# Denominators from the exponentials' accumulator, projections in pairs, and rows normalised ahead, in a two-layer decoder kernel

## The reference, cut to what matters

```python
# routed feed-forward: 64 experts, 3 per row, 128 rows each
logits = xf @ gate_w + gate_b
top_l, top_i = jax.lax.top_k(logits, 3)
gates = softmax(top_l)
pos = (cumsum(one_hot, axis=0) * one_hot).sum(-1) - 1      # place of a row at its expert
# causal attention, 16 heads of 16
score = einsum('bqhd,bkhd->bhqk', q, k) / 16 + m * rel     # then causal mask, softmax, times v
# relative cross attention over a context of 361, 16 heads of 16
attn1 = einsum('bhqd,bhkd->bhqk', rq, rk)
attn2 = einsum('bhqd,qkd->bhqk', rq, rel_k)                # table row = distance clipped to +-32
attn = softmax((attn1 + attn2) / 4)
w1 = einsum('bhqk,bhkd->bhqd', attn, rv)
w2 = einsum('bhqk,qkd->bhqd', attn, rel_v)
x = (w1 + w2) @ Wo + bo
```

## Time and profile before

| | us |
|---|---|
| median of 3 runs (lowest, highest) | 2668.37 (2657.73, 2670.3) |
| profiled execution, its own time | 2665.95 |
| its span, first to last instruction | 2664.2 |
| routing | 545 to 657 |
| causal attention | 1173 to 1403 |
| relative attention | 1407 to 2265 |

### The profile page before, as it was taken

The page is one execution under the profiler, slowest core; times in us unless marked ns, Lnnn a source line. Parts: engine busy times, 40 slices in busy tenths (PEclk is TensorE's granted clock), DMA queues, the critical chain, the costliest instruction groups (busy, mean ns, idle before and its releaser), DMA issues. The chain is left out here.

```text
span 2664.2 us, 52615 instructions
## 1 busy us (share of the span) xinstructions
...
## 2 busy tenths in 40 slices
...
GB/s 83 41 87 68 67 67 67 45 246 102 293 344 341 344 345 344 241 132 1 0 26 106 129 127 136 125 131 127 125 136 126 130 125 54 38 56 0 58 44 41
DMA packets 375990, 339.40 MB, mean 127 GB/s; under 512 B 70226, under 2 KB 351852, under 8 KB 374636
## 3 DMA queue, kind: packets, MB, share of 16 engines
...
## 5 line engine op out<-in xcount | busy, mean ns | idle before, releaser
L2269 ACT COPY rel_probT<-rel_ps_t 121x400 f32<-121x400 f32 x384 | 193.6, 504 | 173.3 <-PE rel_ps_t L2482 173.3
L2281 ACT ACTIVATE rel_prob<-rel_ps_s,rel_nmx 100x361 f32<-100x361 f32 x512 | 263.7, 576 | 2.6 <-DVE rel_nmx L2357 2.4
L2482 PE MATMUL rel_ps_t<-rel_ident,rel_prob 100*121 100x100 f32 x1536 | 239.2, 278 | 6.7 <-ACT rel_probT L2269 6.7
L1378 PEld LDWEIGHTS moe_ps_h<-moe_xeT,moe_w 128*128 128x128 f32 x2048 | 241.5, 194 | 5.1 <-issue 1.9
L2482 PEld LDWEIGHTS rel_ps_t<-rel_ident,rel_prob 100*121 100x121 f32 x1536 | 202.5, 186 | 58.1 <-ACT rel_probT L2269 20.5
L1378 PE MATMUL moe_ps_h<-moe_xeT,moe_w 128*128 128x128 f32 x2048 | 242.0, 277 | 1.3 <-DVE moe_xeT L1543 1.3
L2357 DVE TENSOR_REDUCE rel_nmx<-rel_ps_s 100x2 f32<-100x722 f32 x256 | 232.8, 909 | 8.8
L1378 PE MATMUL moe_ps_y<-moe_w,moe_hT 128*128 128x256 f32 x1024 | 231.5, 379 | 0.0
L2996 PE MATMUL ffd_ps_y<-ffn_w_dT,ffd_oq 128*100 128x256 f32 x384 | 86.2, 386 | 139.8 <-DVE ffd_oq L2941 134.2
L1369 ACT ACTIVATE moe_hT<-moe_ps_h,moe_b 128x128 f32<-128x128 f32 x512 | 142.9, 376 | 138.5 <-PE moe_ps_h L1378 138.2
L1378 PEld LDWEIGHTS moe_ps_y<-moe_w,moe_hT 128*128 128x128 f32 x1024 | 189.6, 190 | 23.2
...
## 6 DMA issues: line engine op xcount, KB each, us to landing
moe_w<-in_L_ffn_w SPq DMA_DIRECT2D x128, 1024.0 KB, 9.5
...
rel_weights<-rel_prob ACTq DMA_DIRECT2D x128, 204.7 KB
...
```

The costliest lines, as they stand in the source:

```text
L1378: return nc.tensor.matmul(out, lhsT, rhs, start=(k == 0), stop=(k == n - 1))
L2269: nc.scalar.copy(probT[:, pg % 2, c], ps_pT).then_inc(s_t_sb, 1)
L2281: last = nc.scalar.activation(prob[:, t.parity, slot, :], ps_s[0:S, j, 0:L], ACT.Exp, bias=nmx[:, slot:slot + 1])
L2482: last = nc.tensor.transpose(ps_pT[:, j, :], prob[:, pt.parity, QUAD * pg + j, c * STEP:c * STEP + R], ident[0:S, 0:S])
```

## The change

Three stages are edited.

- **Routing.** ACT normalises the rows, three groups ahead, from a new tile `shift`; DVE no longer does. The place products are two over 256 columns instead of eight over 64. The zeros go out behind group 2, the experts' weights behind groups 5, 6 and 7.
- **Causal attention.** Rows are normalised and transposed five batch elements ahead (`AHEAD`), and q and k are projected for two at a time, q in one turn and k in the next. The transposes stand behind the projection.
- **Relative attention.** The exponentials write their row sums (`accum_out=den`). DVE inverts and spreads them in g0 (`invert`), `den` turns them with two products against `ident`, and DVE copies them. `vals` holds zeros instead of ones, each head pair sums into its final rows, `swap` and `pick` are gone, and DVE adds `raw` to the distance part (`mixed`) ahead of the product with `rec`. The far sum moves to g0, and PE instead of DVE waits for the DMA. `out` moves from place 14 to 15.

```diff
+                if g == 2:
                     sp.dma_start(b1[:], io["L0_ffn_b1_cols"]).then_inc(s_b1, 16)
                     sp.dma_start(y_rows[1][0:B * S].rearrange("(r p) d -> p r d", p=P),
                                  zeros[:].unsqueeze(1).to_broadcast([P, B * S // P, D])).then_inc(s_spare, 16)
-                elif g <= DEEP:
-                    first_weights(g - 1)
+                if g >= GROUPS - 3:
+                    first_weights(g - (GROUPS - 3))
+            first_weights(3)
...
+                g, far, later = t, t + 2, t + 3
+                if later.within(GROUPS):
+                    if not isinstance(later.i, int) or later.i > 1:
+                        act.wait_ge(s_xg_out[later.parity], 32 * later.half)
+                        act.wait_ge(s_T, 2 * later.i - 2)
+                    for q in range(G):
+                        b = later.i * G + q
+                        last = nc.scalar.activation(xg[:, later.parity, q, :], at(y_nat, b), ACT.Identity,
+                                                    bias=shift[:, bass.ds(b, 1)], scale=rstd[:, bass.ds(b, 1)])
+                    last.then_inc(s_xg, 1)
...
-                    for q in range(G):
-                        mm(ps_place[:, q, :], before[:], mask[:, v, q, :], 0, 2)
-                        last = mm(ps_place[:, q, :], ones[0:S, 0:S], so_far[:, v, q - 1, :] if q else so_far[:, 1 - v, G - 1, :], 1, 2)
+                    mm(ps_place.rearrange("p g e -> p (g e)"), before[:], mask[:, v].rearrange("p g e -> p (g e)"), 0, 2)
+                    last = mm(ps_place.rearrange("p g e -> p (g e)"), ones[0:S, 0:S],
+                              so_far[:, v].rearrange("p g e -> p (g e)"), 1, 2)
...
-    RING = 4
+    RING = 8
+    AHEAD = 5
...
-            def project(n, out, sem):
+            def project(n, pair, sem):
+                two = slice(pair.phase % 4, pair.phase % 4 + 2)
                 for c in range(KC):
                     for k in range(KC):
-                        last = mm(out[:, c, :], w[:, k, n * D + c * P:n * D + (c + 1) * P], xT[:, k, :], k, KC)
+                        last = mm(ps_pair[:, c, :], w[:, k, n * D + c * P:n * D + (c + 1) * P],
+                                  xT[:, k, two, :].rearrange("p b s -> p (b s)"), k, KC)
                 last.then_inc(sem, 1)
 
             def turn(t):
...
-                prev, b, nxt, far = t + -1, t, t + 1, t + 2
+                prev, b, nxt, far = t + -1, t, t + 1, t + AHEAD
                 if nxt.within(B):
                     scores(nxt)
 
+                    latest = nxt.i + AHEAD - 1
+                    pe.wait_ge(s_xT_sb, min(latest, B) if isinstance(latest, int) else latest)
                     for k in range(KC):
-                        last = mm(ps_v, xT[:, k, :], w[:, k, 2 * D:3 * D], k, KC)
+                        last = mm(ps_val, xT[:, k, nxt.phase % 4, :], w[:, k, 2 * D:3 * D], k, KC)
                     last.then_inc(s_v, 1)
-                if far.within(B):
-                    pe.wait_ge(s_xn, far.i + 1)
-                    for c in range(KC):
-                        last = nc.tensor.transpose(ps_xT[:, c, :], xn[:, far.phase, c * P:(c + 1) * P], ident[0:S, 0:S])
-                    last.then_inc(s_xT, 1)
                 if prev.within(B):
                     natural(prev)
                 if b.within(B):
                     weightsT(b, nxt, 0)
                     weightsT(b, nxt, 1)
+                pair = t + (2 + t.phase % 2)
+                if pair.within(B):
+                    p = pair.half(2)
+                    if t.phase % 2:
+                        pe.wait_ge(s_xT_sb, 2 * p + 2)
+                        if not isinstance(p, int) or p > 0:
+                            pe.wait_ge(s_k_sb, p)
+                        project(1, pair, s_q)
+                    else:
+                        pe.wait_ge(s_q_sb, p + 1)
+                        project(0, pair, s_k)
                 if far.within(B):
-                    pe.wait_ge(s_xT_sb, far.i + 1)
+                    pe.wait_ge(s_xn, far.i + 1)
                     if nxt.within(B):
                         pe.wait_ge(s_v_sb, nxt.i + 1)
-                    project(0, ps_k, s_k)
-                    project(1, ps_q, s_q)
+                    if not isinstance(far.i, int) or far.i > 0:
+                        pe.wait_ge(s_xT_sb, far.i)
+                    for c in range(KC):
+                        last = nc.tensor.transpose(ps_xT[:, c, :], xn[:, far.phase, c * P:(c + 1) * P], ident[0:S, 0:S])
+                    last.then_inc(s_xT, 1)
                 if b.within(B):
                     sums(b)
 
-            rounds(pe, turn, -2, 2, B - 2, B + 1, RING)
+            rounds(pe, turn, -AHEAD, 2, B - 6, B + 1, RING)
...
-        PLACES = [[0], [1], [2], [3], [4], [5], [6], [7], [], [8], [9], [10], [11], [12], [13], []]
+        PLACES = [[0], [1], [2], [3], [4], [5], [6], [7], [], [8], [9], [10], [11], [12], [], [13]]
...
-                    sp.dma_start(by_dist[:], bass.AP(p_rows.tensor, p_rows[v].offset,
-                                                     [[NH * PW + 1, S], [PW, NH], [1, ND]])).then_inc(s_pdist, 16)
+                    sp.dma_start(by_dist[:, :, 1:ND], bass.AP(p_rows.tensor, p_rows[v].offset + 1,
+                                                              [[NH * PW + 1, S], [PW, NH], [1, ND - 1]])).then_inc(s_pdist, 16)
...
-                                                bias=nmx[:, slot:slot + 1])
+                                                bias=nmx[:, slot:slot + 1],
+                                                accum_out=den[:, t.parity, slot:slot + 1])
...
-                    nc.vector.reciprocal(rec[:], two(what)).then_inc(s_job_sb[n % 2], 1)
+                    nc.vector.tensor_copy(rec[:], two(what)).then_inc(s_job_sb[n % 2], 1)
                 elif what == "w2":
+                    dve.wait_ge(s_att, b.i + 1)
+                    nc.vector.tensor_tensor(mixed[:], two(what), raw[:], ALU.add).then_inc(s_mix, 1)
+                    dve.wait_ge(s_mix, b.i + 1)
                     wait_emptied(dve, t, "den")
-                    nc.vector.tensor_tensor(attT[:], two(what), rec[:], ALU.mult).then_inc(s_job_sb[n % 2], 1)
+                    nc.vector.tensor_tensor(attT[:], mixed[:], rec[:], ALU.mult).then_inc(s_job_sb[n % 2], 1)
                 elif what == "out":
...
+            def invert(b):
+                dve.wait_ge(s_p, GROUPS * b.i + (GROUPS + 1))
+                nc.vector.reciprocal(den_rec[:].rearrange("p (c j e) -> p c j e", c=KC, e=2),
+                                     den[:, b.parity].rearrange("p (c e j) -> p c j e", c=KC, e=2)).then_inc(s_den, 1)
+                dve.wait_ge(s_den, b.i + 1)
+                if not isinstance(b.i, int) or b.i > 0:
+                    wait_filled(dve, b, "den")
+                nc.vector.tensor_copy(den_wide[:], den_rec[:].unsqueeze(2).to_broadcast([S, NH, HD])).then_inc(s_wide, 1)
...
                     maxima(t, g, 0)
+                    if g == 0 and prev.within(B):
+                        invert(prev)
...
-                        if g == 2 and k == 1 and prev.within(B):
+                        if g == 0 and k == 2 and prev.within(B):
                             dve.wait_ge(s_far, prev.i + 1)
-                            dve.wait_ge(s_pdist, 16 * prev.i + 16)
+                            if not isinstance(prev.i, int) or prev.i > 0:
+                                wait_filled(dve, t + -1, "d1")
                             nc.vector.reduce_sum(by_dist[:, :, 0], far[:], AX.X).then_inc(s_far_sum, 1)
...
                     pe.wait_ge(s_far_sum, b.i + 1)
+                    pe.wait_ge(s_pdist, 16 * b.i + 16)
...
-                    pe.wait_ge(s_att, b.i + 1)
-                    for e in range(2):
-                        last = mm(two(what), swap[:, e, :], raw[:].rearrange("p (c e) s -> p e c s", e=2)[:, e], e, 2)
+                    pe.wait_ge(s_wide, b.i + 1)
+                    for c in range(KC):
+                        last = mm(two(what)[:, c, :], den_wide[:, c * HC:(c + 1) * HC, :].rearrange("p h d -> p (h d)"),
+                                  ident[0:S, 0:S], 0, 1)
                 elif what == "w2":
-                    for e in range(2):
-                        nc.tensor.matmul(two(what), pick[:, e, :], raw[:].rearrange("p (c e) s -> p e c s", e=2)[:, e],
-                                         start=(e == 0), stop=False)
                     wait_emptied(pe, t, "d1")
                     for q in range(QUAD):
                         last = nc.tensor.matmul(two(what), tab_v_wide[:, q, :],
                                                 distT[:].rearrange("p (c q) s -> p q c s", c=KC)[:, q],
-                                                start=False, stop=(q == QUAD - 1))
+                                                start=(q == 0), stop=(q == QUAD - 1))
                 else:
                     wait_emptied(pe, t, "w2")
...
```

(4 more changed lines are left out.)

134 lines of the change are left out of this document (67 added, 67 removed).

## The result

The changed kernel takes 2652.03 us (median of 4 runs, 2650.7 to 2653.38) against 2667.11 us for the kernel before (4 runs, 2657.73 to 2670.3). The ratio is 0.9949, 95% interval 0.9929 to 0.9968: faster by 14 us by the ratio and 15 by the medians, half of the forecast, and a gain of only half a percent. The profiled execution took 2650.7 us, its span is 2649.0 us.

The account below looks back on a forecast made before the run. Taken as bounds: DVE in routing, PE in causal attention, mostly a PE-ACT loop in relative attention. Terms -6 - 9.5 - 14 = -29.5 us from the profiled 2665.95 gave 2637 us; own range 2620 to 2652, with rivals 2606 to 2662.

Parts of the forecast that it names:

- +4 us of used-up slack: Relative attention: upper bound of its sum if each read costs its whole 0.19 us record and slack is used up.
- Reads of the accumulator, +0.37 us a turn: Relative attention: each read adds 0.09 us to an exponential, costing 0.18 us in g1, 0.12 in g0, 0.07 in g2.
- The rival with reads: Relative attention: reads cost their whole record, ACT loop loses in three groups, stage +4 us, kernel 2655 us; chance 0.13.
- Far sum, -0.55: Relative attention, g2: moving the far sum to g0 removes PE's wait for it, 0.55 us a turn.
- `pick`, -0.21: Relative attention, g3: without `pick`, T1 comes 0.64 us earlier and the group ends 0.21 us earlier.
- Causal attention, 6.25 us a batch element: Causal attention: 6.25 us instead of 6.71, 13 us saved over 29, start +3.5 us, sum -9.5 us.
- The loop of 6.14 us: Causal attention: the loop through the score banks becomes the next bound, at 6.14 us.
- about 0.15 us late: Causal attention: in turns that project k, ACT's spreading of k makes the next scores 0.15 us late.
- Routing: Routing: groups take 9.2 us instead of 10.78, start 4 us later, shorter place products save about 0.5; sum -6 us.
- my slower rival: Relative attention: PE's clock falls because of new gaps; kernel 13 us slower (2681 us) at 5.2% half-clock time; chance 0.10.
- PE as the bound of relative attention: Relative attention, a rival: PE sets the time, 1.34 us a turn saved, 43 us, kernel 2606 us; chance 0.08.
- No wait for the transfer of `rel_by_dist`: Relative attention: PE, now waiting for this DMA itself, was to show no wait for it; a wait would prove the forecast wrong.

Follow-up runs that it names:

- x1: Changed kernel without the accumulator reads in relative attention, the tile of sums held constant (output scale wrong): 2627.82 us in one run.
- x9: x5 with accumulator reads added to its exponentials, whose sums nobody reads: 2666.32 us in one run.
- x5: Kernel before with only the far sum moved to g0, PE waiting for the now shorter `rel_by_dist` transfer: 2643.07 us, ratio 0.9926.
- x2: Changed kernel with `out` back at place 14 and nothing at place 15: 2646.53 us in one run.
- x4: Changed kernel with k projected in the odd turn and q in the even one in causal attention: 2647.12 us, ratio 0.9922.
- x7: Changed kernel with eight unused PE products ahead of each of the routing's last three table sums: 2648.52 us in one run.
- x8: Changed routing with the edits of x6 and x7, causal attention of x4, relative attention of x5: 2623.73 us, ratio 0.9836 to the kernel before.
- x6: Changed kernel with ACT's copies ahead of its row normalising in the routing, from group 1 on: 2639.49 us in one run.

## Why the prediction was wrong

The sign was right, and 2652 us lies at the upper end of the forecast's own range of 2620 to 2652 (the rivals took the stated range to 2606 and 2662). The sum of -29.5 us was twice what came (-15.2 in span). Two sums of the prediction don't come out as written: the bounds of its three terms, taken half way each, give about 2625 to 2653 us (2656 with the +4 us of used-up slack), and turns of 6.14 and 6.29 us have a mean of 6.22, not 6.25. By its steps:

- **Reads of the accumulator, +0.37 us a turn: the step that failed most.** The price of a pair was right (0.19 measured, 0.18 forecast). Wrong was where it is paid: I gave g2 "some slack" (0.07), without a row for it, and g3 nothing, because PE set T2 there. Measured by x1 and x9 every group pays, 0.70 to 0.74 us a turn, 11 us more than forecast. g2 had only 0.04 us of slack and pays 0.15, and g3 pays 0.15 through a wait that the prediction doesn't have, that of the next scores for the last exponential. The rival with reads had the direction, but by its own mechanism (a whole record of 0.19 us each) it was wrong: a read adds 0.09.
- **Far sum, -0.55: too small.** x5 shows -0.75. I took the idle time of the products; that of their weight loads was 0.69. Worth 6 us more than forecast, which hid half of the first miss; that the two misses had opposite signs was luck.
- **`pick`, -0.21: right** (-0.18 with the rest). But `out` at place 15, which I had counted only in g3, cost 0.13 us a turn, in g0 above all (x2).
- **Causal attention, 6.25 us a batch element.** The loop of 6.14 us came close, 6.25 in turns of q and, in x4, in all. The term that failed is "about 0.15 us late" for ACT's spreading of k: 0.53 in every second turn. That is 0.24 us a batch element saved instead of 0.46, or 6.8 us in 29 instead of 13. From the norm before to the bias of element 2 it is 30.0 us instead of 25.2 (1194.39 - 1164.42 against 1194.01 - 1168.83), so the start cost 4.8 us instead of 3.5; from the last bias to the norm behind it 12.8 instead of 14.7, which gave 1.9 back. Both ends vary with the same code, though: the start took 27.2 to 30.0 us in seven traces of the change and 25.2 to 27.8 in three without, by the means 2.9 us more, and the end took 12.8 us in x5 too, which has the old code. So the forecast of the start stands, and no gain at the end is shown.
- **Routing.** 9.25 us a group and 3.7 us at the start were forecast (9.2 and 4). What I left out is the end: in this trace PE stood idle longer before its second-last sum, and the clock stood at 0.54 for the last two, some 2 to 3 us. That the change makes this more likely (five traces of six, against one of three before) is not shown by so few. It was the mechanism of my slower rival, but in the routing and not where I had put it; in relative attention the clock stayed at 1.00. The Trainium skill (TensorE: Matmul & The Clock Gate, What's actually happening) says that a gate sets PE's clock by how busy PE was recently. x7 and x8, where more work made the third-last and the second-last sum faster, agree.
- **PE as the bound of relative attention: wrong**, as I had held. PE's busy share fell from 97.1 to 95.8% while the turn fell by 0.9%, and in x9, with reads alone, it rose to 98.8% in a turn 0.74 us longer than that of x5. The Trainium skill's rule that matmul busy time is a bad metric (Trainium Kernel Development and Optimization, Performance Expectations) held here.
- **No wait for the transfer of `rel_by_dist`: right in the loop, not at the end.** None appears in the loop of the changed kernel or of x5. For the last batch element PE waits once, 1.5 us in this trace, 0.6 in x6 and not at all in x4, x5 and x7:

```profile
2241.15 1.57 PE L2476 MATMUL rel_ps_m<-rel_ident,rel_by_dist 100*128 100x100 f32 x8 [1.47 <-DMA rel_by_dist<-rel_weights]
```
